# The gate's silu made from tanh: a function of exp's table set on ScalarE, and one product more on VectorE

## What is computed

```python
hs, gate = proj[:, :DI], proj[:, DI:]
dA  = exp(A[None, :, None, :] * dt[:, :, :, None])
dBu = (dt[:, :, :, None] * Bm[:, None, :, :]) * hs[:, :, :, None]
h = dA_t * h + dBu_t
y = einsum('bdn,bn->bd', h, C_t)
y = y + hs * D[None, :, None]
y = y * silu(gate)
x = x + einsum('bdl,hd->blh', y, Wout) + linear(gelu(ff_gate) * ff1)
```

## Time and profile before

| | |
|---|---|
| median of three runs | 1242.43 us (1240.92 to 1244.25) |
| profiled execution | 1240.33 us, of it the span of the program 1238.5 us |
| busy: PE / VectorE / ScalarE / POOL | 936.5 / 1053.9 / 761.0 / 995.9 us |
| second phase | from about 239 us to the end |
| table loads in ScalarE's blocks of the second phase | 83, at 1283 ns each |

### The profile page before, as it was taken

How to read it: one execution, slowest core, us unless ns; L and a number is a source line. 1 busy time by engine, 2 the same in 40 slices (tenths; PEclk the granted TensorE clock), 3 DMA queues, 4 the chain that set the end, 5 groups by cost and what they waited for, 6 DMA issues and landing times.

```text
span 1238.5 us, 17003 instructions
## 1 busy us (share of the span) xinstructions
PE 936.5 (76%) x4304; PEld 581.2 (47%) x4304; DVE 1053.9 (85%) x1205; ACT 761.0 (61%) x1097; POOL 995.9 (80%) x783
## 2 busy tenths in 40 slices
PE   4979888376767696977676969776768697767798
PEld 3656555144444454544344545444445454434454
DVE  7877867589888899899888998998889989988994
ACT  4888786655666556666555656665546566666451
POOL 4342534697998899999888999998889999998893
PEclk9999999787887899889788999988889899888899
DMA  8675768861110219222111292211213822211100
GB/s 279 209 256 189 275 248 305 312 230 47 52 35 27 77 59 334 89 71 68 39 44 59 80 323 86 65 69 38 70 35 93 314 82 65 69 35 68 35 1 35
DMA packets 53187, 150.53 MB, mean 122 GB/s; under 512 B 5728, under 2 KB 14048, under 8 KB 50016
## 3 DMA queue, kind: packets, MB, share of 16 engines
q1 hardware_dynamic: 53088, 149.41, 34.9%
HBM read 111.37 MB, written 38.01 MB: 121 GB/s over the span
## 4 chain that ended last, share of the span: by engine, by line
POOL 53%; issue 17%; DVE 4%; ACT 3%; PE 3%; POOLq 1%; DVEq 0%
POOL dbu L926 41%; POOL hp L934 12%; DVE da L980 1%; DVE gate_bf L995 1%; PE mm L1023 1%; DVE prod L949 1%; DVE hp L980 1%; PE yT L1101 1%; PE da L1023 1%; ACT gate_bf L875 1%; ACT L876 1%; ACT L875 1%; ACT L871 1%; PE mm L1080 0%; POOLq L925 0%
## 5 line engine op out<-in xcount | busy, mean ns | idle before, releaser
L885 ACT ACTIVATE da<-unit,neg_a 128x512 f32<-128x512 f32 x512 | 340.1, 685 | 270.2 <-DVE prod L949 254.8
L926 POOL TENSOR_TENSOR dbu<-unit,b_head 128x512 f32<-128x512 f32 x384 | 496.0, 1327 | 7.0 <-POOLq L99 3.5
L980 DVE TENSOR_TENSOR_SCAN da<-da,dbu 128x512 f32<-128x512 f32 x320 | 384.6, 1218 | 77.5 <-ACT da L885 69.5
L1101 PE MATMUL yT<-ident,prod 128*128 128x128 f32 x1280 | 214.9, 296 | 127.9 <-DVE prod L949 127.1
L1101 PEld LDWEIGHTS yT<-ident,prod 128*128 128x128 f32 x1280 | 160.8, 150 | 242.1 <-DVE prod L949 186.4
L934 POOL TENSOR_TENSOR hp<-hp,c_head 128x512 f32<-128x512 f32 x160 | 206.1, 1288 | 75.2 <-DVE hp L980 75.0
L980 DVE TENSOR_TENSOR_SCAN hp<-da,dbu 128x512 f32<-128x512 f32 x192 | 231.3, 1205 | 19.9 <-ACT da L885 8.9
L1059 PE MATMUL mm<-xn_b,w_sb 128*128 128x512 fp8e4 x512 | 166.7, 475 | 92.9 <-ACT gate_bf L893 92.9
L926 POOL TENSOR_TENSOR dbu<-unit,b_all 128x512 f32<-128x512 f32 x128 | 175.2, 1398 | 0.0
L949 DVE TENSOR_TENSOR prod<-da,c_head 128x512 f32<-128x512 f32 x224 | 149.1, 666 | 0.0
L1059 PEld LDWEIGHTS mm<-xn_b,w_sb 128*128 128x128 fp8e4 x512 | 59.4, 118 | 165.2 <-issue 142.9
(11 more groups left out here) (106 smaller groups left out, 1257.4 us busy)
## 6 DMA issues: line engine op xcount, KB each, us to landing
unit<-unit_d SPq DMA_DIRECT2D x32, 768.0 KB, 4.3
unit_d<-dt_du SPq DMA_DIRECT2D x32, 512.0 KB, 2.9
wf<-in_wffn SPq DMA_DIRECT2D x12, 1024.0 KB, 5.8
c_head<-bc_d SPq DMA_DIRECT2D x24, 512.0 KB, 5.4
b_head<-bc_d SPq DMA_DIRECT2D x18, 512.0 KB, 5.3
unit_d<-hsd SPq DMA_DIRECT2D x32, 256.0 KB, 4.3
w_sb<-w_d SPq DMA_DIRECT2D x64, 128.0 KB, 3.6
wgate<-in_win_gate SPq DMA_DIRECT2D x32, 256.0 KB, 2.7
```

Of the source, the lines that this page charges most:

```text
L885: nc.scalar.activation(da[n % SLOTS][:, :], unit[:, k % 2, 0, :], ACT.Exp, scale=neg_a[:, k, n:n + 1]).then_inc(da_ready, 1)
L926: nc.gpsimd.tensor_tensor(dbu[:, n % DBUS, :], unit[:, k % 2, 1, :], b_all[n // NS][:, n % NS, :], ALU.mult).then_inc(dbu_ready, 1)
L980: nc.vector.tensor_tensor_scan(state, da[n % SLOTS][:, :], dbu[:, n % DBUS, :], 0.0, ALU.mult, ALU.add).then_inc(scanned, 1)
L1101: ins = nc.tensor.matmul(yT[k % 2][:, t * P:(t + 1) * P], product[:, t * P:(t + 1) * P], ident[:, :], start=False, stop=last, is_transpose ...
```

## The change

silu(x) is written as x (1 + tanh(x/2)) / 2. ScalarE's block applies tanh to half of the gate, which lies in one set with exp (`exp_and_others`); the set is loaded once at the start of the phase and again only after a gelu. A new function of VectorE, `gate_silu`, makes (tanh + 1) times the gate in one operation behind state 5, from `sg` in SBUF and the gate's bank in PSUM, and raises `sg_ready`, which ScalarE raised before. The factor 1/2 goes into the copy of y.

```diff
-                nc.scalar.activation(y_t[:, :], yT[k % 2][:, :], ACT.Copy).then_inc(y_t_ready, 1)
+                nc.scalar.activation(y_t[:, :], yT[k % 2][:, :], ACT.Copy, scale=0.5).then_inc(y_t_ready, 1)
...
-                        nc.scalar.activation(sg[:, :], mm[plan[(before, "gate", 0)][0]][:, :], ACT.Silu).then_inc(sg_ready, 1)
+                        nc.scalar.activation(sg[:, :], mm[plan[(before, "gate", 0)][0]][:, :], ACT.Tanh, scale=0.5).then_inc(tanh_ready, 1)
                         if before < FFN_UNITS:
...
-                        nc.scalar.preload_act_table_set("natural_log_exp_and_others")
+                            nc.scalar.preload_act_table_set("exp_and_others")
...
+            nc.scalar.preload_act_table_set("exp_and_others")
             run_units(act, body)
...
-            nc.scalar.activation(sg[:, :], mm[plan[(KU - 1, "gate", 0)][0]][:, :], ACT.Silu).then_inc(sg_ready, 1)
+            nc.scalar.activation(sg[:, :], mm[plan[(KU - 1, "gate", 0)][0]][:, :], ACT.Tanh, scale=0.5).then_inc(tanh_ready, 1)
...
+            def gate_silu(u, k):
+
+                dve.wait_ge(tanh_ready, u + 1)
+                nc.vector.scalar_tensor_tensor(out=sg[:, :], in0=sg[:, :], scalar=1.0, in1=mm[plan[(k, "gate", 0)][0]][:, :],
+                                               op0=ALU.add, op1=ALU.mult).then_inc(sg_ready, 1)
...
+                    if n == 5 and not first:
+                        gate_silu(u - 1, (k - 1) % KU)
                     if n == GATED and not first:
...
             times_c(B - 1, KU - 1, N - 1)
+            gate_silu(B * KU - 1, KU - 1)
             gated(B * KU - 1, KU - 1)
```

More of the change, by code:

```diff
@@ L686, in block_b @@
         y_t_ready, back_mm, y2_ready = sem("y_t_ready"), sem("back_mm"), sem("y2_ready")
-        gate_mm, sg_ready = sem("gate_mm"), sem("sg_ready")
+        gate_mm, tanh_ready, sg_ready = sem("gate_mm"), sem("tanh_ready"), sem("sg_ready")
         ffn_mm, ffn_copied, gelu_ready = sem("ffn_mm"), sem("ffn_copied"), sem("gelu_ready")
```

## The result

The changed kernel takes 1264.98 us (median; 1263.46 to 1266.09), beside 1241.68 us for the kernel before on the same chip: ratio 1.0183, 95% interval 1.0164 to 1.0203. The forecast was 1236 us and the range ended at 1262. What happened is the first rival, the slower one.

A forecast was written before the change was run, and what follows sets the result against it. POOL was taken to set the pace, with ScalarE's block on the path in gelu units. -32.1 + 4.32 s with s = 6 gave -6 us: 1240.33 to 1234, 1236 us on the median's scale; range 1214 to 1262.

The forecast's parts named there:

- ScalarE's block: At state 6 of 20 gelu units: one load fewer, so the exp behind it comes 1.28 us earlier.
- the first rival, the slower one: Gelu products locked out wherever POOL has not paused: 9 to 13 units, +7 to +24 us, 1249 to 1267 us, chance 0.28.
- the 13 units: Gelu units where POOL's wait ahead of hp 7, only 0.64 to 0.84 us, would vanish, putting the gelu product at risk.
- the new product costs nothing: In gelu units its 0.75 us on VectorE runs within the 1.56 us of wait left; uncovered, up to 24 us.
- the price of a lockout: Per at-risk unit, gelu product kept out while POOL runs four operations: loss 2.44 us, against gain 1.88 if let in.
- the gain of 1.88: Per at-risk unit, gelu product let in at POOL's next boundary: 1.28 us plus 0.60 us less waiting.
- The formula: Whole-kernel change: six gains of 1.28 us, 13 of 1.88, plus 4.32 us per lockout: -32.1 + 4.32 s.
- the count s: Number of lockouts among the 13 at-risk gelu units, put at 6, giving a change of -6 us.
- the choice of six units by the width of a pair of operations: POOL pairs ahead of hp 7: four of 2.52 us or more lock out, two of five at 2.50 or 2.51.
- those called safe: Four at-risk units whose POOL pair ahead of the wait took 2.49 us or less: none locks out.
- the faster rival: Lockout almost nowhere: 0 to 3 of the at-risk units, -32 to -19 us, 1210 to 1223 us, chance 0.25.
- the safe units: Unit 5 of each batch and unit 4 of batches 1 and 2 keep a POOL wait: six gains of 1.28 us.

The follow-up runs named there:

- experiments 5 and 6: 5: changed kernel, POOL's hp 7 waits for the gelu product in units 1 to 5, 1199.83 us; 6: kernel before with the same wait, 1228.30 us.
- Experiment 7: Kernel of experiment 2 with the new VectorE product moved behind state 6 instead of state 5; 1224.73 us.
- experiment 2: Changed kernel, but in units 1 to 5 POOL's dbu 10 also waits for scan 7; 1210.98 us.

## Why the prediction was wrong

**Right: ScalarE's block.** It is one load shorter, and POOL's waits ahead of `hp` 7 are gone in the 13 units. VectorE's wait at state 6 is 0.83 us in unit 3 of batch 1 and in seven more; over all 20 it is 0.58 to 1.43, where 0.8 to 1.0 was said from a unit with 2.84 us before (others had up to 3.44). With the wait of `hp` 7 in both kernels, the change is worth 26.3 us behind the first phase (experiments 5 and 6), 1.31 us per gelu unit where 1.28 were put down.

**Right: the new product costs nothing.** PE starts the feed-forward group of that bank without a wait (unit 3 of batch 1):

```profile
599.82 1.89 PE L1069 MATMUL mm<-xn_b,w_sb 128*128 128x512 fp8e4 x8
```

The tail stays: from the start of VectorE's last products to its last `y` (line 962) it is 8.32 us before and after. Experiment 7 shows what the cover was worth, 13.7 us (up to 24 was the bound).

**Right: the price of a lockout; the fit of the sum is in part luck.** A let-in against a lockout was put at 4.32 us, of it +2.44 against before. In batch 1 the products of units 2 and 3 start 33.40 us apart, at 569.25 and 602.65; before 31.00 us, at 559.76 and 590.76:

```profile
569.25 6.07 DVE L1002 TENSOR_TENSOR gate_bf<-gate_bf,up_bf 128x1536 bf16<-128x1536 bf16 x1
```

```profile
559.76 1.67 DVE L995 TENSOR_TENSOR gate_bf<-gate_bf,up_bf 128x1536 bf16<-128x1536 bf16 x1
```

That is +2.40 us a unit. In experiment 2 the same two stand 29.57 us apart, 1.43 less than before: the gain of 1.88 that was put down for a product let in, less the pause of 0.44 us that POOL keeps there. The formula with s = 13 gives +24.1 us, and 23.3 were measured, but its terms fit less well than its sum. Unit 4 of batch 1, put down as a gain of 1.28 us, was locked out and lost 2.86 (from its product to the next 37.29 us, 34.43 before). Unit 4 of batch 2 made up for most of it with a gain of 3.03 (31.40 us, 34.43 before), and the stretches from the products of units 5 to the next batch's first product, or to the end, gained 7.0 us together where 5.1 were put down. With s = 0 the formula gives -32.1, and experiment 2 measured -31.8, again with less from the 13 units (19.4 us where 24.4 were put down) and more from the other six (11.8 where 7.7 were).

**Wrong: the count s.** The step that failed is "What marks it in POOL's rows is that successive operations overlap", and with it the choice of six units by the width of a pair of operations. The overlap decides nothing. In unit 3 of batch 0 the product (353.56 to 359.63) was locked out between POOL operations that were as narrow as those called safe, 2.49 us for the pair ahead and 2.47 for the pair behind:

```profile
351.44 2.49 POOL L927 TENSOR_TENSOR dbu<-unit,b_head 128x512 f32<-128x512 f32 x2
353.89 1.26 POOL L935 TENSOR_TENSOR hp<-hp,c_head 128x512 f32<-128x512 f32 x1
355.12 1.25 POOL L927 TENSOR_TENSOR dbu<-unit,b_head 128x512 f32<-128x512 f32 x1
356.34 2.47 POOL L927 TENSOR_TENSOR dbu<-unit,b_all 128x512 f32<-128x512 f32 x2
```

In the ten profiles, where POOL had not just paused, the pair that ends with the operation running at the product's start took 2.48 to 2.53 us when the product was let in and 2.48 to 2.57 us when it was locked out.

The distance since POOL's last wait tells them apart: it was 17 operations in ten of the 13 units, 75 in the other three, and 35 in the one lockout known before. So s is 13, not 6, as the slower rival had it. The clip that was let in at 594.07, the evidence against the slower rival, stood two operations after the pause at 590.34 and said nothing about a POOL that never pauses. The evidence for the faster rival, that ten of the units follow a pause for scan 10, did not hold either: that pause is 17 operations back, too far.

**Wrong in a small part: the safe units.** Units 5 kept a pause. Unit 4 of batches 1 and 2 did not: POOL's last pause lay ahead of `dbu` 1, 12 and 11 operations before the product, and the profile names no engine that ended it ("issue"). The first product was locked out, the second let in. POOL and VectorE in the second:

```profile
877.37 3.72 POOL L927 TENSOR_TENSOR dbu<-unit,b_head 128x512 f32<-128x512 f32 x3 [3.43 <-issue]
```

```profile
891.78 1.16 DVE L1002 TENSOR_TENSOR gate_bf<-gate_bf,up_bf 128x1536 bf16<-128x1536 bf16 x1
```

## What to carry to other kernels

A wait that looks like lost time can be what lets another engine in, so when a change takes a wait away, look at what runs on the shared resource just then. Where VectorE has an operation with two SBUF inputs beside a POOL that runs without a break, make POOL wait for that operation on purpose if POOL waits for something a little later anyway: here that turned +23 us into -43. One case of a rare event in a trace does not tell which of its features causes it; count each candidate (here operations since the last pause) before choosing one.

## What the runs showed of the hardware

The gelu product is let in at POOL's next boundary up to 11 operations after POOL last stood still (127 of 127), now and then at 12 and 13 (4 of 19), and from 14 on never (0 of 54); then it runs only when POOL stands still, and ends 0.8 us after POOL's last operation (1.1 us for the larger product of units 5). VectorE's products with one input in PSUM ran at 0.67 to 0.68 us in the mean, beside a POOL without pauses too (lines 950 and 955 above).

The Trainium skill, SBUF — State Buffer, section SBUF: two separate sides, says that a VectorE instruction with two SBUF inputs and a GpSimd instruction that reads SBUF exclude each other, and that the first to start has the shared ports for its whole instruction. The trace agrees as long as POOL has paused lately (the product ends 0.8 us after POOL's running operation, and POOL's next takes 1.98 us instead of 1.27); after a long run it differs, for the product then waited through two to five POOL instructions that started after its own start.

Why the distance counts stays open. The Trainium skill, GPSIMD Engine Reference, section Instruction dispatch, has the cores of POOL go on one by one, and cores that drift apart after a common start would fit. That is not shown: no row here shows the single cores, and the overlap of the rows, which was taken for that drift, did not tell the two cases apart.
